# Block transposes on VectorE and products on POOL for the attention's value output, and all norms' scaling on ScalarE

## What is computed

```
def mha(x, W_in, b_in, W_out, b_out, mask):          # 16 heads of 16
    q, k, v = split(x @ W_in.T + b_in, 3)
    a = softmax(q @ k.T / sqrt(16) + mask)           # per head; mask = triu(ones, k=1)
    return concat_heads(a @ v) @ W_out.T + b_out
h = LN(x)
fused = w[0] * mha(h @ proj_local, ..., windows of 128) + w[1] * mha(h @ proj_global, ..., windows of 256)
x1 = x + LN(LN(fused) * gamma + beta)
xn2 = LN(x1)
top1 = argmax(softmax(xn2 @ w_router))               # 32 experts, capacity 320 rows each
out = x1 + LN(xn2 + gate * (silu(b @ w_gate) * (b @ w_up)) @ w_down)   # b: the rows sent to the expert
```

## Time and profile before

| | |
|---|---|
| median of 3 runs (lowest to highest) | 1819.14 us (1817.94 to 1822.35) |
| the profiled execution: time, span | 1818.58 us, 1816.8 us |
| mean granted TensorE clock | 0.968 of full speed |
| busy, share of the span: PE, DVE, ACT, POOL | 90%, 68%, 55%, 49% |

### The profile page before, as it was taken

One profiled execution on the slowest core, in us unless ns is written; L12 is line 12 of the kernel. 1 busy time (PEld: TensorE's weight loads), 2 busy tenths in 40 slices (PEclk: granted clock), 3 DMA queues, 4 the chain that ended last, 5 costly groups with the idle time before them and its releaser, 6 DMA issues.

```text
span 1816.8 us, 43072 instructions
## 1 busy us (share of the span) xinstructions
PE 1636.8 (90%) x14472; PEld 1184.8 (65%) x14472; DVE 1226.7 (68%) x3673; ACT 993.6 (55%) x2251; POOL 884.3 (49%) x1173
## 2 busy tenths in 40 slices
PE   5779999999999999999999999999999846999993
PEld 3457777777776676766676776777776634666662
DVE  2446777777777776777777777777777534777773
ACT  2356666666666666666666666666666531111210
POOL 3224545445445555545554444444444341666665
PEclk9789999999999999999999999999999967999997
DMA  6985555555555555555555555555555202444540
GB/s 138 222 181 98 95 96 97 96 95 96 97 94 96 96 96 94 95 94 94 93 92 91 91 93 94 94 92 94 92 84 97 67 13 74 146 138 140 153 126 10
DMA packets 254346, 183.59 MB, mean 101 GB/s; under 512 B 30116, under 2 KB 252775, under 8 KB 254142
## 3 DMA queue, kind: packets, MB, share of 16 engines
q1 hardware_dynamic: 245150, 176.22, 48.9%
q0 software_dynamic: 7168, 3.73, 1.2%
q10 hardware_dynamic: 1824, 1.06, 0.2%
HBM read 55.78 MB, written 38.04 MB: 52 GB/s over the span
## 4 chain that ended last, share of the span: by engine, by line
PE 59%; POOL 17%; issue 8%; DVE 6%; SPq 4%; ACT 3%; DVEq 2%; DMA 1%; POOLq 0%; ACTq 0%
PE bank L1147 11%; PE bank L1275 7%; PE bank L1184 5%; PE bank L1178 4%; PE bank L1129 4%; PE bank L1116 4%; PE bank L1137 3%; POOL out L632 3%; POOL zb L627 3%; PE bank L1175 3%; PE bank L1108 3%; PE bank L1104 3%; PE bank L1154 3%; SPq L422 2%; POOL ybuf L583 2%
## 5 line engine op out<-in xcount | busy, mean ns | idle before, releaser
L883 DVE TENSOR_REDUCE mx<-bank 128x2 f32<-128x512 f32 (+1 forms) x768 | 513.3, 685 | 134.1 <-PE bank L1175 87.2
L674 ACT ACTIVATE pt<-bank 128x512 f32<-128x512 f32 x768 | 448.2, 601 | 160.2 <-PE bank L1116 130.2
L550 POOL TENSOR_TENSOR rest<-x,parts 128x512 f32<-128x512 f32 x128 | 148.5, 1160 | 295.7 <-ACT x L688 295.7
L1147 PE MATMUL bank<-xnT,weff 128*128 128x256 f32 x1024 | 247.4, 385 | 2.4 <-ACT x L688 1.7
L1178 PE MATMUL bank<-stack 96*128 96x256 bf16 x1024 | 198.9, 276 | 20.6 <-DVE mx L883 19.6
L688 ACT ACTIVATE parts<-bank,bqk 128x256 bf16<-128x256 f32 x256 | 107.5, 471 | 173.4 <-PE bank L1147 160.4
L1147 PEld LDWEIGHTS bank<-xnT,weff 128*128 128x128 f32 x1024 | 185.9, 191 | 23.8 <-ACT x L688 2.1
L555 POOL TENSOR_TENSOR parts<-rest,parts 128x512 bf16<-128x512 f32 x128 | 148.4, 1160 | 107.7 <-DVE parts L871 107.7
L1116 PE MATMUL bank<-stack 100*128 100x128 bf16 x2048 | 198.9, 219 | 0.0
L1116 PEld LDWEIGHTS bank<-stack 100*128 100x128 bf16 x2048 | 158.9, 98 | 12.5
L1178 PEld LDWEIGHTS bank<-stack 96*128 96x128 bf16 x1024 | 79.5, 98 | 125.2 <-issue 57.4
(11 more groups left out here) (149 smaller groups left out, 3144.3 us busy)
## 6 DMA issues: line engine op xcount, KB each, us to landing
stack<-parts SPq DMA_DIRECT2D x384, 128.0 KB, 6.7
stack<-parts SPq DMA_DIRECT2D x768, 64.0 KB, 2.6
slots_scratch<-zeros SPq DMA_DIRECT2D x5, 2080.0 KB, 11.9
erows<-slots_scratch SPq DMA_DIRECT2D x64, 130.0 KB
xr<-x SPq DMA_DIRECT2D x32, 256.0 KB, 7.2
out<-obuf SPq DMA_DIRECT2D x32, 256.0 KB, 2.1
ew<-w_gate SPq DMA_DIRECT2D x32, 256.0 KB, 3.2
ew<-w_up SPq DMA_DIRECT2D x32, 256.0 KB, 3.5
```

Of the source, the lines that this page charges most:

```text
L550: pool.tensor_tensor(rest[:, j % 2, :], x32[:, j % 2, :], parts[:, j, 0, :], ALU.subtract).then_inc(rest_ready, 1)
L674: act.activation(pt[:, u % 8, :], S2[u % 2][:, :], ACT.Exp).then_inc(p_ready, 1)
L883: dve.reduce_max(dst, src, AX.X).then_inc(s1_read, 1)
L1147: last = pe.matmul(bank[:, t * WIN:(t + 1) * WIN], weff[:, b, c, qk * D + t * P:qk * D + (t + 1) * P], xnT[:, par, c, :], start=(c == 0), ...
```

## The change

- VectorE transposes each group from PV to `otok` in blocks of 32 x 32 (`unfold`), at the unit in which the group is computed. After every second group (a "chunk") it takes the reciprocals of the sums.
- POOL multiplies (`normalise`, one per chunk, four per window, on 256 elements per partition). Its places in POOL's queue are in the diff.
- VectorE transposes the product's blocks back into `OnT` (`fold`), at units 11 and 14 for the local chunks, at 18 for global chunk 0, and at 2 of the next step for global chunk 1.
- The six groups of transposes on TensorE, ScalarE's copies `values_out` and `onT_out`, and VectorE's old `normalise` are gone. The bank TR has three uses per step in place of nine.
- Rows of `wo` and `bv` are loaded in the order that the blocks have: 32 transfers on ScalarE's queue at the start in place of 4.
- Norms 0 and 3 are scaled on ScalarE, in the units where VectorE did it; `inv_std` does four operations for them in place of two. The statistics of xn2 wait for ScalarE.
- `split_l` moves from unit 9 to 12, `mT_l` from 12 to 14, `mT_g` from 1 to 2, `top` from 3 to 4, `gate` from 5 to 6.

```diff
-        TR_USES = [("mT_g", 2, mT_ready[1], 1, 0), ("n_g0", 3, on_ready[1], 2, 0), ("n_g1", 3, on_ready[1], 2, 1),
-                   ("oT_g", 3, onT_ready[1], 1, 0), ("op", 3, f_ready, 1, 0), ("mT_l", 1, mT_ready[0], 1, 0),
-                   ("n_l0", 2, on_ready[0], 2, 0), ("n_l1", 2, on_ready[0], 2, 1), ("oT_l", 2, onT_ready[0], 1, 0)]
+        TR_USES = [("mT_g", 2, mT_ready[1], 1, 0), ("op", 3, f_ready, 1, 0), ("mT_l", 1, mT_ready[0], 1, 0)]
         PJ_USES = [("x2T", 4, x2T_ready, 1, 0), ("xnT", 0, xnT_ready, 1, 0), ("lg", 4, lg_ready, 1, 0), ("p0", 0, x32_ready, 4, 0),
                    ("p1", 0, x32_ready, 4, 1), ("cs", 4, cs_read, 1, 0), ("p2", 0, x32_ready, 4, 2), ("p3", 0, x32_ready, 4, 3),
                    ("v0", 1, v_ready, 2, 0), ("v1", 1, v_ready, 2, 1)]
-        AT = {"split_g": 0, "x2T": 0, "xnT": 0, "mT_g": 1, "lg": 2, "o_norm": 2, "p0": 3, "n_g0": 3, "top": 3, "p1": 5, "n_g1": 5,
-              "gate": 5, "oT_g": 7, "cs": 7, "op": 9, "split_l": 9, "p2": 10, "p3": 12, "mT_l": 12, "f1": 12, "v0": 15, "stats_y": 15,
-              "n_l0": 16, "z": 17, "n_l1": 18, "norm0": 18, "v1": 19, "stats_x1": 19, "oT_l": 20, "xn2": 21, "stats_xn2": 23}
+        AT = {"split_g": 0, "x2T": 0, "xnT": 0, "fold_g1": 2, "mT_g": 2, "lg": 2, "o_norm": 2, "p0": 3, "top": 4, "p1": 5,
+              "gate": 6, "cs": 7, "op": 9, "p2": 10, "fold_l0": 11, "split_l": 12, "p3": 12, "f1": 12, "fold_l1": 14, "mT_l": 14,
+              "v0": 15, "stats_y": 15, "z": 17, "norm0": 18, "fold_g0": 18, "v1": 19, "stats_x1": 19, "xn2": 21, "stats_xn2": 23}
         GROUP_AT = {3: 0, 5: 1, 7: 2, 9: 3, 13: 4, 17: 5, 21: 6}
...
-        ACT_NORMS = (1, 2, 4)
+        ACT_NORMS = (0, 1, 2, 3, 4)
...
+            def normalise(b, chunk, w):
+                wait(pool, rden_ready, w, 4, 2 * b + chunk)
+                wait(pool, onT_ready[b], back(w), 2, chunk)
+                pool.tensor_tensor(On[:, b, chunk, :].rearrange("p (n s d) -> p s n d", s=2, d=HD),
+                                   otok[:, b, chunk, :, :].rearrange("p s (n m) -> p s n m", m=32)[:, :, :, 0:HD],
+                                   rden[:, b, chunk, :, :].unsqueeze(3).to_broadcast([P, 2, WIN // 32, HD]), ALU.mult).then_inc(on_ready, 1)
...
             def step(s, par):
                 a, b, c, d, f = stages(s)
                 nxt = back(s, -1)
+                if d:
+                    normalise(1, 1, d)
                 if a:
                     remainder(0, a)
                 if f:
...
                 if a:
                     low_part(0, a)
                     remainder(1, a)
+                if c:
+                    normalise(0, 0, c)
+                if a:
                     low_part(1, a)
                 if f:
                     pool.wait_ge(zeroed, 16 * ZDMAS)
...
                         pool.indirect_dma_start(
                             out=slots_d, out_offset=bass.IndirectOffsetOnAxis(ap=slot_u[:, q:q + 1], axis=0),
                             in_=xrow[:, q, :], in_offset=None, bounds_check=NSLOT - 1, oob_is_err=False).then_inc(scat, 16)
+                if c:
+                    normalise(0, 1, c)
                 if d:
                     inv_std(1, d)
                 if a:
...
                     wait(pool, xn2_ready, back(d))
                     pool.wait_ge(xr_in[1 - par], xr_count(d))
                     pool.tensor_tensor(x1[:, :, :], ybuf[:, :, :], xr[:, 1 - par, :, :], ALU.add).then_inc(x1_ready, 1)
+                if c:
+                    normalise(1, 0, c)
                 if a and (nxt[0] is not None or nxt[1] < NW):
                     inv_std(0, nxt)
                 if d:
...
-                act.dma_start(bv[:, 2 * b:2 * b + 2], v_).then_inc(wo_in, 16)
+                for h in range(4):
+                    for half in range(2):
+                        lo, at = 64 * half + HD * h, 32 * h + HD * half
+                        act.dma_start(bv[at:at + HD, 2 * b:2 * b + 2], v_[lo:lo + HD, :]).then_inc(wo_in, 16)
+                        act.dma_start(wo[at:at + HD, 2 * b:2 * b + 2, :], o_.rearrange("(c p) n -> p c n", p=P)[lo:lo + HD, :, :]
+                                      ).then_inc(wo_in, 16)
                 act.dma_start(bqk[:, b, :], k_).then_inc(wo_in, 16)
-                act.dma_start(wo[:, 2 * b:2 * b + 2, :], o_.rearrange("(c p) n -> p c n", p=P)).then_inc(wo_in, 16)
                 act.dma_start(bo[:, b, :], c_.partition_broadcast(P)).then_inc(wo_in, 16)
...
-            def values_out(g, c):
-                wait(act, pv_full, c, GROUPS, g)
-                b = g // 4
-                wait(act, nrm_full[b], back(c), 2, 1)
-                act.activation(OT[:, b, g % 4, :], PV[:, 0:WIN], ACT.Copy).then_inc(ot_ready, 1)
...
+            def first_norm(w, par):
+                wait(act, xnT_full, back(w))
+                norm(0, xn, xw[:, par, :, :], xn_ready, w)
+            first_norm((None, 0), 0)
...
-            def onT_out(b, w):
-                wait(act, onT_full[b], w)
-                wait(act, o_full, back(w))
-                act.activation(OnT[:, b, :, :].rearrange("p t n -> p (t n)"), TR[:, :], ACT.Copy).then_inc(onT_ready[b], 1)
...
+                    if a and exists(back(a, -1)) and k == AT["norm0"] + 2:
+                        first_norm(back(a, -1), 1 - par)
+                    if d and k == AT["xn2"]:
+                        wait(act, x2T_full, back(d))
+                        norm(3, xn2, x1, xn2_ready, d)
...
-            def normalise(b, q, w):
-                wait(dve, nrm_full[b], w, 2, q)
-                src = TR[:, :].rearrange("p (h m) -> p h m", m=32)
-                dve.reciprocal(rden[:, b, :], src[:, :, HD])
-                dve.drain()
-                wait(dve, onT_full[b], back(w))
-                dve.tensor_tensor(On[:, b, q, :].rearrange("p (h d) -> p h d", d=HD), src[:, :, 0:HD],
-                                  rden[:, b, :].unsqueeze(2).to_broadcast([P, NH, HD]), ALU.mult).then_inc(on_ready[b], 1)
+            def unfold(g, w):
+                b, chunk, half = g // 4, g // 2 % 2, g % 2
+                wait(dve, pv_full, w, GROUPS, g)
+                if half == 0:
+                    wait(dve, on_ready, back(w), 4, 2 * b + chunk)
+                dve.transpose(otok[:, b, chunk, half, :], PV[:, 0:WIN]).then_inc(pv_read, 1)
+                if half == 1:
+                    dve.drain()
+                    dve.reciprocal(rden[:, b, chunk, :, :], otok[:, b, chunk, :, :].rearrange("p s (n m) -> p s n m", m=32)[:, :, :, HD]
+                                   ).then_inc(rden_ready, 1)
+            def fold(b, chunk, w):
+                if chunk == 0:
+                    wait(dve, o_full, back(w))
+                wait(dve, on_ready, w, 4, 2 * b + chunk)
+                dve.transpose(OnT[:, b, chunk, :], On[:, b, chunk, :]).then_inc(onT_ready[b], 1)
...
                         split_maxima(0, b)
                     if f and k == AT["top"]:
                         route_top(f)
-                    for q in range(2):
-                        if d and k == AT[f"n_g{q}"]:
-                            normalise(1, q, d)
-                        if c and k == AT[f"n_l{q}"]:
-                            normalise(0, q, c)
+                    if c and k in GROUP_AT:
+                        unfold(GROUP_AT[k], c)
+                    if d and k == LAST_GROUP_AT:
+                        unfold(GROUPS - 1, d)
+                    if d and k == AT["fold_g1"]:
+                        fold(1, 1, d)
+                    for chunk in range(2):
+                        if c and k == AT[f"fold_l{chunk}"]:
+                            fold(0, chunk, c)
+                    if c and k == AT["fold_g0"]:
+                        fold(1, 0, c)
                     for j in range(4):
                         if a and k == AT[f"p{j}"] + 3:
                             mid_part(j, a)
...
                     if d and k == AT["stats_x1"]:
                         wait(dve, x1_ready, d)
                         stats(3, x1, d)
-                    if first and k == AT["norm0"] + 2:
-                        first_norm(nxt, 1 - par)
                     if d and k == AT["xn2"]:
-                        wait(dve, x2T_full, back(d))
-                        wait(dve, o_norm, back(d))
-                        norm(3, xn2, x1, xn2_ready, d)
+                        wait(dve, ln_rstd[3], d)
                         dve.tensor_copy(xrow[:, :, MEAN], mv[:, 3, :, 0])
                         dve.tensor_copy(xrow[:, :, RSTD], rstd[:, 3, :])
                     if d and k == AT["stats_xn2"]:
-                        dve.drain()
+                        wait(dve, xn2_ready, d)
...
-                wait(pe, ot_ready, c if g else back(c), GROUPS, (g - 1) % GROUPS)
+                wait(pe, pv_read, c if g else back(c), GROUPS, (g - 1) % GROUPS)
...
-            def norm_T(b, q, w, s):
-                wait_read(pe, TR_USES, f"n_{'lg'[b]}{q}", s, 1)
```

(56 more changed lines are left out.)

## The result

The changed kernel takes 2028.6 us (median of 4 runs, 2026.1 to 2029.1) against 1820.1 (1817.9 to 1822.4): ratio 1.114, 95% interval 1.112 to 1.116. The direction was the forecast one; the size was not. The forecast was 1898, and the result lies above the range's upper end of 1935.

The account below looks back on a forecast made before the run. Prediction: TensorE's stream bounds half A, a four-engine chain half B. Half A 2.0 us less, half B 4.2 more: +2.2 per step, +69 over 31 steps, +10 at the start, 1818.6 to 1898 us; range 1770 to 1935.

Parts of the forecast that it names:

- Transposes off TensorE: Both halves lose three transpose groups; 1.5 us off the first half plus its 0.82 us gap; VectorE's transposes 0.35 each.
- rival (c): VectorE becomes the bound, transposes taking 0.7 instead of 0.35: one more microsecond per step, 1935 us; chance 0.10.
- half A: Step from x2T (transposes of xn2) to the output projection's end, TensorE streaming: 23.4 us, forecast 21.4.
- Route_top one unit later still precedes p1: In half A: moving route_top a unit later was given no cost of its own.
- The allowance of 0.3: Half A: 0.3 us, between 0 and 1, for late unfold(2), route_slot and a POOL product, with row_scores(9) waiting.
- split_l: Half B, unit 12: VectorE's four instructions wait for POOL's products; +1.0 us, 1.5 if all held, 0 if none.
- The `pow` row: Counter-evidence on split_l: VectorE's `mparts` took 0.19 us amid POOL's 0.69 us two-element `pow`, implying no hold.
- fold_g0: Half B, unit 18: waits for POOL's product behind x1, delaying stats_x1 to 3.35 us after x1 from 0.99; +2.4 us.
- half B: Step from projection end to next x2T, set by a chain over four engines: 20.5 us, forecast 24.7.
- Rival (b): fold_g0 doesn't decide, half B stays as it is and half A's gain counts: 1757 us, faster; chance 0.19.
- Norm 3 on ScalarE: Half B's end: stats_x1 to x2T grows from 3.67 to 4.5 us, one exponential queued behind the norm; +0.8 us.
- The start: Kernel start: 28 more small transfers of wo and bv on ScalarE's queue delay the first steps; +10 us.

Follow-up runs that it names:

- experiment 10: Experiment 9's kernel plus four unread matmuls on TensorE ahead of the row scores of units 17 and 18: 1774.0 us, ratio 0.975.
- experiment 4: Changed kernel with top back at unit 3 and gate at 5: 1964.0 us, ratio 1.078.
- experiment 2: Changed kernel with fold_g0 at unit 20 in place of 18: 1935.5 us, ratio 1.065.
- experiment 7: Two runs: kernel before with only norms 0 and 3 moved to ScalarE, 1844.9 us; changed kernel with them back on VectorE, 1984.3 us.
- Experiment 6: Changed kernel with rows of wo and bv ordered beforehand, so four transfers load them in place of 32: 2019.0 us, ratio 1.110.
- Experiment 5: Changed kernel with ten overwritten matmuls added on TensorE in the gap before mT_l, its two waits there swapped: 1976.8 us, ratio 1.087.
- experiment 9: Changed kernel with split_l, mT_l, top and gate back, fold_g0 at 20, four transfers for wo and bv, norms 0 and 3 on VectorE: 1795.6 us.
- the four together: Changed kernel with split_l, mT_l, top and gate back, fold_g0 at unit 20, and wo and bv loaded by four transfers: 1831.7 us, ratio 1.006.

## Why the prediction was wrong in size

Step by step, in the forecast's order.

- **Transposes off TensorE.** Right: 0.44 us busy each on VectorE, 0.36 from start to start, not 0.7, so rival (c) falls with VectorE at 69%. What half A gains by it, together with the gap ahead of mT_g, is 1.4 us in experiment 10, 0.6 under the 2.0 that the forecast gave to half A.
- **Half A: the sentence "Route_top one unit later still precedes p1".** This is the first step that failed. It asked whether the result would be late for TensorE and not what POOL runs at the new place. The row `hot` shows 2.25 us for 0.39, a hold of 1.9, and experiment 4 gives 1.2 us per step for it in the part of half A where it stands (2.1 with the clock behind x2T). The allowance of 0.3 was for a late row_scores(9), where TensorE waits 0.43, and not for this.
- **split_l.** The mechanism was right and the size was off: held were three of four, not one, and the delay of part 2 is 1.4 us, not 1.0. The `pow` row that spoke against it was no evidence for 512-element operations, as the text itself suspected. The Trainium skill, "SBUF — State Buffer", Who interferes with whom, has a POOL instruction and a VectorE one that has two SBUF inputs or runs in a 2-port mode block each other for the whole instruction. The trace agrees here with three holds (1.05, 1.25 and 1.27 us for 0.2), though no row shows in what mode L887 and L891 run, which have one input each. By that rule the prediction had put the term at 1.5, and it measured 1.4.
- **fold_g0.** Right: 3.16 us from x1 to its statistics (3.35 forecast), 2.4 us of half B by experiment 2. Rival (b), that it doesn't decide, falls.
- **Norm 3 on ScalarE.** The mechanism was right and the term of 0.8 too small. In the changed kernel the way from stats_x1 to x2T is 4.95 us, not 4.5, which is 1.3 more than before, as TensorE's scores in it wait for exponentials queued behind two norms (0.62 and 0.90 us). The forecast had one such exponential. That experiment 7 gives 0.8 as a total in the kernel before is luck: 1.7 more in half B less 0.7 in half A.
- **The start.** The first weight activations are 7.3 us later (23.59 against 16.25). The first x2T is 13.3 later, but that holds a first slow half B as well. Experiment 6 gives 9.6 for the transfers by the medians and 3 to 5 by the profiles. The term of 10 had the right order, and that it was exact is not shown.
- **What the sum did not contain: TensorE's clock.** This is the largest miss, 2.45 us of the step. Every gap was priced by its length. Half B by the trace: stats_y starts 2.5 us later, counted from the projection's end (13.4 against 10.8), of which split_l's 1.4 is one part. The other 1.1 is v0 at half clock, 3.52 us for 1.94, which makes maximum(15) late (VectorE waits 1.04 us for it ahead of those statistics). In half A, x2T and xnT, issued behind the gaps of half B, take 1.06 us each where they took 0.63 and 0.60; from x2T to the first value products it is 3.01 us (488.40 to 491.41) instead of 1.66 (519.60 to 521.26), 1.35 more. Experiment 5 gives 1.9 us of a 50.8 us step (1.2 in B, 0.6 in A over the steps measured by halves) by filling one gap alone.

Added up for one step, against the forecast's +2.2: `hot` 1.2, the clock 1.1 in half B and 1.35 in half A, the smaller gain of half A 0.6, split_l 0.4, norm 3's queue 0.45 and fold_g0 -0.2 come to +7.1; the step followed here shows 7.05 (24.46 and 26.5 against 23.4 and 20.5). The forecast counted 31 full steps, the trace has 28; the draining three gain 5.5 us (fewer transposes stand in their serial path, but no run shows that this is the reason). Both are small beside the rest, and so are the forecast's slips in arithmetic: 31 times 2.2 is 68 and not 69, and rival (c), one more microsecond per step, comes to 1929, not 1935.

One reading in the forecast was incomplete. "TensorE work removed there buys nothing by itself" holds where the clock stays up: half B is 20.3 us in experiment 10 and was 20.4. It can also have a price, since removed work turns stream into gap, and the clock may fall behind the gap: the same kernel without the eight matmuls has a half B of 21.5. That also explains why undone waits returned time in places where they did not stand, and part of why the four together returned less than their sum.

What stays open: which of ScalarE's two norms costs the time, why the clock falls behind the same two gaps in 16 steps of experiment 9 and not in 12, and how the clock's price is shared between the gap at unit 14 and those at units 18 to 22, as only the first was filled in the changed kernel itself.

## What to carry to other kernels

When an instruction moves by a unit, ask not only who waits for it but what runs beside it on an engine that can hold it: here a 0.4 us pair became 2.3 us, and 1.2 of the 1.9 went into the step. When a wait opens a gap on TensorE, price the gap and then the next few microseconds of matmuls at half clock, and check in how many steps that happens. When a total agrees with a term, look at the parts: one term here was right only as the difference of two others. And where such a gap can't be removed, matmuls that nobody reads can be cheaper than idleness: eight per step were worth 1.2% of this kernel's time.

## What the hardware showed beyond the forecast

- More matmuls made two kernels faster: 2028.6 to 1976.8 us with ten per step, 1795.6 to 1774.0 with eight.
- The granted clock fell to its lower level behind one gap of 2.46 us, and in experiment 9 in 16 of 28 steps (0.57 and 0.58 in two stretches of 2 us) behind two gaps of 0.92 and 0.82 us that start some 1.5 us apart. In the other 12 steps it stayed at its upper level behind the same two gaps (0.91 and 0.82 us, v1 at 1.94). The fall and the return both come inside a run of matmuls: v0's four are slow throughout, the scores behind them run at full speed again within 4 us.
- A block transpose of 128 x 256 fp32 values, from PSUM or from SBUF, costs VectorE 0.44 us, about as much as a multiplication of that size from PSUM (0.42).
- Of VectorE's small operations beside a 512-element POOL operation, the bf16 writes from one fp32 input (L887, L891, L934) were held to the end of POOL's, as were the two-input ones (L893, L946). A block transpose from SBUF was not: 0.42 us at 522.30, inside POOL's 1.16 us from 521.85.
